# 24 instead of 20 ranges of edges scattered to blocks; low source numbers spread by DMA; attribute products in 64-row halves

## What is computed

```python
h = relu(layernorm(x))
x = x + gcn(relu(gcn(h, W1, b1)), W2, b2)       # two GCN convolutions over the edges
h = relu(layernorm(x))
msg  = relu(concat(h[row], edge_attr) @ L1_W1 + b1)     # one message per edge
agg  = segment_sum(msg, col) / max(count, 1)
out  = x + relu(concat(h, agg) @ L1_W2 + b2)
```

## Time and profile before

| | |
|---|---|
| median of 3 runs | 2926.35 us (2925.55 to 2926.58) |
| the profiled execution | 2923.46 us |
| its span in the profile | 2921.6 us |
| mean granted clock of TensorE | 0.954 |
| busy share of the span | PE 87%, POOL 63%, DVE 55%, ACT 35% |

### The profile page before, as it was taken

The page is one execution under the profiler, slowest core; times in us unless marked ns, Lnnn a source line. Parts: engine busy times, 40 slices in busy tenths (PEclk is TensorE's granted clock), DMA queues, the critical chain, the costliest instruction groups (busy, mean ns, idle before and its releaser), DMA issues.

```text
span 2921.6 us, 53392 instructions
## 1 busy us (share of the span) xinstructions
PE 2554.8 (87%) x18818; PEld 2059.8 (71%) x18819; DVE 1612.8 (55%) x3028; ACT 1021.3 (35%) x2891; POOL 1842.2 (63%) x1747
## 2 busy tenths in 40 slices
PE   1756578999999995999996599999999999999997
PEld 0104357888778894888885487877878777777786
DVE  7889897888766556000002654544545455454556
ACT  6504133566667764000000233333333333333331
POOL 2852363677887771756661277777777777777750
PEclk9997699999999997989998699999999999999999
DMA  9102221332434442746563222232222232222321
GB/s 372 37 6 74 77 63 59 133 124 106 150 116 153 177 180 89 237 155 239 210 231 113 89 76 79 76 90 77 79 76 80 79 88 79 76 79 76 90 49 48
DMA packets 111653, 327.75 MB, mean 112 GB/s; under 512 B 33282, under 2 KB 71527, under 8 KB 104855
## 3 DMA queue, kind: packets, MB, share of 16 engines
q10 hardware_dynamic: 6624, 147.72, 12.6%
q0 software_dynamic: 58352, 93.38, 12.4%
q1 hardware_dynamic: 46377, 82.75, 8.1%
HBM read 197.11 MB, written 126.61 MB: 111 GB/s over the span
## 4 chain that ended last, share of the span: by engine, by line
PE 71%; DVE 18%; issue 5%; POOL 2%; ACT 2%; DMA 1%; DVEq 1%; ACTq 0%; SPq 0%; POOLq 0%
PE ps_feat L889 12%; PE ps_node L889 12%; PE ps_extra L1036 7%; PE ps_sum L997 7%; PE ps_pre L990 6%; DVE region_c L1680 4%; DVE region_c L1676 4%; PE ps_node L1020 3%; PE ps_node L1024 3%; PE ps_pre L877 3%; PE ps_sum L1020 2%; PE ps_feat L1020 2%; PE ps_sum L1024 2%; PE ps_feat L1024 2%; PE ps_turn L1012 2%
## 5 line engine op out<-in xcount | busy, mean ns | idle before, releaser
L630 POOL DMA_INDIRECT rows<-table,region_a x928 | 895.6, 965 | 384.7 <-issue 262.4
L648 POOL DMA_INDIRECT permuted<-edge_rows_of,slot_of_edge x640 | 728.1, 1138 | 323.0 <-issue 150.6
L889 PE MATMUL ps_node<-region_a,region_b 128*128 128x256 bf16 x3528 | 450.5, 273 | 1.8 <-ACT region_b L1126 1.8
L1849 DVE TENSOR_SCALAR region_b<-ps_turn,consts 128x512 f32<-128x512 f32 (+1 forms) x280 | 191.6, 684 | 461.8 <-PE ps_turn L1012 418.4
L889 PE MATMUL ps_feat<-region_a,region_b 128*128 128x256 bf16 x3528 | 445.8, 273 | 0.0
L889 PEld LDWEIGHTS ps_node<-region_a,region_b 128*128 128x128 bf16 x3528 | 341.4, 97 | 45.4 <-ACT region_b L1126 2.0
L889 PEld LDWEIGHTS ps_feat<-region_a,region_b 128*128 128x128 bf16 x3528 | 342.3, 98 | 44.1
L1680 DVE TENSOR_TENSOR region_c<-iota_key,region_c 128x1568 bf16<-128x1568 f16 (+1 forms) x324 | 354.1, 1093 | 0.0
L1676 DVE TENSOR_TENSOR region_c<-iota_units,region_c 128x1024 bf16<-128x1024 bf16 x324 | 224.3, 692 | 136.5 <-PE ps_turn L877 91.3
L1164 ACT ACTIVATE region_a<-ps_pre 128x392 bf16<-128x392 f32 x384 | 190.8, 497 | 215.8 <-PE ps_pre L877 207.9
L1036 PE MATMUL ps_extra<-region_b 128*128 128x128 f32 x1960 | 265.2, 275 | 0.0
(11 more groups left out here) (255 smaller groups left out, 3747.1 us busy)
## 6 DMA issues: line engine op xcount, KB each, us to landing
counts<-region_a ACTq DMA_DIRECT2D x24, 3136.0 KB
region_a<-counts ACTq DMA_DIRECT2D x22, 3136.0 KB
permuted<-region_b SPq DMA_DIRECT2D x21, 833.0 KB, 23.6
region_a<-permuted SPq DMA_DIRECT2D x20, 833.0 KB, 4.7
region_a<-attr_t_in SPq DMA_DIRECT2D x58, 256.0 KB
rows<-table,region_a POOLq DMA_INDIRECT x928
edge_rows_of<-edge_cols_in POOLq DMA_DIRECT2D x20, 544.0 KB
permuted<-edge_rows_of,slot_of_edge POOLq DMA_INDIRECT x640
```

What stands on the lines that cost most here:

```text
L630: nc.gpsimd.indirect_dma_start(rows[:, s, j * D:(j + 1) * D], None, tables[2], bass.IndirectOffsetOnAxis(ap=message_rows[:, c * TC + j:c * ...
L648: nc.gpsimd.indirect_dma_start(permuted, bass.IndirectOffsetOnAxis(ap=slot_of_edge[:, r * RT + k:r * RT + k + 1], axis=0), edge_rows_of[:, ...
L889: ins = mm(strip_bank(buf), parts[:, h, k], counts[buf][:, h], start=(h == 0 and k == 0), stop=(h == SB - 1 and k == PARTS - 1), skip_grou ...
L1849: v.tensor_scalar(source_hot[u % 2][:, 0:n], ps_turn[:, 0:n], partition, None, ALU.is_equal).then_inc(B["source"], 1)
```

## The change

- `RANGES` 20 becomes 24. Twelve pairs instead of ten, 768 scatters instead of 640 (`PACED` 16 and 8 ranges), 25 clearing transfers instead of 21, and 200 chunks (800 gathers) instead of 232 (928). A pair has 16 chunks; the last has 24.
- The low source numbers no longer go through `spread`. Once a range, PE transposes them (`turn_lows`), ACT copies the result out and stores it to DRAM, and four DMAs on ACT's queue (`load_lows`) bring it to all partitions as bfloat16 in `spread_lo`, from which `source` reads. `spread_lo` is one buffer, filled for one range after the other, a part as soon as its units are compared.
- `products_of` makes two chunks at a time, each as two matmuls of 64 rows by 256 columns, whose results lie in different PSUM banks.
- SP loads the blocks of the next pair when ACT has staged and DVE has prepared the old ones, and no longer when DVE has compared them. Some semaphores are merged.

```diff
-RANGES = 20
+RANGES = 24
+LO_UNITS = 4
+LO_TURNED_AT = (7, DU + 10)
+LO_LOADED_AT = ({DU - 4: (0, 1), DU - 2: (2,), DU: (3,)}, {2 * DU - 1: (0, 1), 2 * DU: (2,), 2 * DU + 1: (3,)})
-PAIR_TURNS = 3
+PAIR_TURNS = 2
-PACED = (13, 7)
+PACED = (16, 8)
...
                 def products_of(k, c):
-                    s = c % SLOTS
-                    if s % HALF == 0:
-                        pe.wait_ge(attr_loaded[s // HALF], (k * PAIR_TURNS + c // SLOTS) * 16 + 16)
-                    pe.wait_ge(rows_added, k * PAIR_CHUNKS + c + 1)
-                    mm(ps_pre[s % 2][:], attr[:, s], edge_w[:].rearrange("p j d -> p (j d)"), start=True, stop=True).then_inc(pre_ready, 1)
+                    pe.wait_ge(rows_added, k * PAIR_CHUNKS + c + 2)
+                    if c % HALF == 0:
+                        pe.wait_ge(attr_loaded[c % SLOTS // HALF], (k * PAIR_TURNS + c // SLOTS) * 16 + 16)
+                    for q in range(2):
+                        for half in range(2):
+                            part = slice(half * P // 2, (half + 1) * P // 2)
+                            last = mm(pre_halves[:, half, q], attr[part, (c + q) % SLOTS],
+                                      edge_w[part, half * 2:half * 2 + 2].rearrange("p j d -> p (j d)"), start=True, stop=True)
+                    last.then_inc(pre_ready, 2)
...
+                def turn_lows(k, r):
+                    pe.wait_ge(B["prepared"], k * 2 + r + 1)
+                    pe.wait_ge(B["lo_evicted"], k * 2 + r + 1)
+                    mm(ps_turn[0:SB, 0:P], block_lo[r][:, 0:SB], ident_bf[:], start=True, stop=True).then_inc(B["lo_turned"], 1)
...
-                    pe.wait_ge(B["source"], k * PAIR_UNITS + u + 1)
-                    for j in range(n):
-                        last = mm(ps_turn[:, j * P:(j + 1) * P], block_lo[r][:, b0 + j:b0 + j + 1].to_broadcast([P, P]), ident_bf[:],
-                                  start=True, stop=True)
-                    last.then_inc(B["spread"], 1)
...
+                def store_lows(k, r, stored=True):
+                    act.wait_ge(B["lo_turned"], k * 2 + r + 1)
+                    if stored:
+                        act.wait_ge(B["lo_stored"], (k * 2 + r) * 16)
+                    nc.scalar.activation(lo_turned[:], ps_turn[0:SB, 0:P], ACT.Copy).then_inc(B["lo_evicted"], 1)
+                    act.wait_ge(B["lo_evicted"], k * 2 + r + 2)
+                    act.dma_start(lo_dram[r].rearrange("(b e) -> b e", e=P), lo_turned[:]).then_inc(B["lo_stored"], 16)
+
+                def load_lows(k, r, i, sourced=None):
+                    act.wait_ge(B["lo_stored"], (k * 2 + r) * 16 + 16)
+                    if sourced is not None or i >= 2:
+                        act.wait_ge(B[f"lo_loaded_{i % 2}"], (k * 2 + r) * 32 + i // 2 * 16)
+                    if sourced is not None:
+                        act.wait_ge(B["source"], sourced)
+                    first, end = i * LO_BLOCKS * P, min((i + 1) * LO_BLOCKS, SB) * P
+                    act.dma_start(spread_lo[:, first:end], lo_dram[r:r + 1, first:end].to_broadcast([P, end - first])
+                                  ).then_inc(B[f"lo_loaded_{i % 2}"], 16)
...
-                    v.tensor_scalar(source_hot[u % 2][:, 0:n], ps_turn[:, 0:n], partition, None, ALU.is_equal).then_inc(B["source"], 1)
+                    v.tensor_scalar(source_hot[u % 2][:, 0:n], lows, partition, None, ALU.is_equal).then_inc(B["source"], 1)
```

More of the change, by code:

```diff
@@ L99 @@
 assert SEG % BANKS == 0
-assert DT % (SLOTS * TC) == 0 and LAST_CHUNKS == 2 * SLOTS and RANGES % 2 == 0 and DU % 2 == 0 and sum(UNIT_TILES) == SB and RT % 2 == 0
+assert DT % (SLOTS * TC) == 0 and LAST_CHUNKS % SLOTS == 0 and RANGES % 2 == 0 and DU % 2 == 0 and sum(UNIT_TILES) == SB and RT % 2 == 0
 assert DT * P >= RANGE_ROWS
@@ L292, in build @@
         ps_extra = ps("ps_extra", [P, 512])
-        ps_pre = [ps("ps_pre0", [P, 512]), ps("ps_pre1", [P, 512])]
+        pre_banks = ps("pre_banks", [P, 1024])
+        ps_pre = [pre_banks[:, k * 512:(k + 1) * 512] for k in range(2)]
+        pre_halves = pre_banks[:].rearrange("p (k h c) -> p k h c", k=2, h=2)
         ps_turn = ps("ps_turn", [P, 512])
@@ L338, in build @@
         rows_staged = [sem("rows_staged_0"), sem("rows_staged_1")]
-        scattered = [sem(f"scattered_{j}") for j in range(4)]
-        lo_ready = sem("lo_ready")
-        hi_ready = sem("hi_ready")
+        scattered = [sem(f"scattered_{j}") for j in range(2)]
+        hot_ready = sem("hot_ready")
         hist_used = sem("hist_used")
@@ L1042, in pair_of @@
                         c = chunk_of(u, chunks)
-                        if c is not None and (not last or c + 2 < chunks):
+                        if c is not None and c % 2 == 0 and (not last or c + 2 < chunks):
                             products_of(k, c + 2)
                         if u < PAIR_UNITS:
-                            spread(k, u)
+                            turn_attr(k, u)
                         if c is not None:
@@ L1052, in pair_of @@
                             block_sums(k, u - 2)
+                        if u == LO_TURNED_AT[0]:
+                            turn_lows(k, 1)
+                        if u == LO_TURNED_AT[1] and not last:
+                            turn_lows(k + 1, 0)
+                turn_lows(0, 0)
                 pe.wait_ge(B["msgs"], 2)
                 products_of(0, 0)
-                products_of(0, 1)
                 with pe.Fori(0, PAIRS - 1) as k:
@@ L1250, in pair_of @@
                             block_message(k, u - 1)
+                        if u == LO_TURNED_AT[0] + 1:
+                            store_lows(k, 1)
+                        for i in LO_LOADED_AT[0].get(u, ()):
+                            load_lows(k, 1, i, k * PAIR_UNITS + (min(LO_UNITS * (i + 1), DU) + 1))
+                        if u == LO_TURNED_AT[1] + 1 and not last:
+                            store_lows(k + 1, 0)
+                        for i in LO_LOADED_AT[1].get(u, ()):
+                            if not last:
+                                load_lows(k + 1, 0, i, k * PAIR_UNITS + (DU + min(LO_UNITS * (i + 1), DU) + 1))
+                for j in range(2):
+                    act.wait_ge(scattered[j], RANGES // 2 * RT * 16)
+                store_lows(0, 0, False)
+                for i in range(LO_PARTS):
+                    load_lows(0, 0, i)
                 stage_attr(0, 0)
@@ L1432, in _ @@
                         dve.wait_ge(hist_used, i * 2 + s + 1)
[L1433 removed]
+                        for hot, of, n in ((hot_lo, dst_lo, P), (hot_hi, dst_hi, NB)):
                             v.tensor_tensor(hot[:, s], iota_bf[:, None, 0:n].to_broadcast([P, HT, n]),
                                             of[:, bass.ds(i * (2 * HT) + s * HT, HT)].unsqueeze(2).to_broadcast([P, HT, n]),
[L1436 removed]
+                                            ALU.is_equal).then_inc(hot_ready, 1)
                 dve.wait_ge(count_ready, 1)
@@ L1845, in source @@
                 def source(k, u):
-                    n = unit_tiles(u % DU)[1] * P
-                    dve.wait_ge(B["spread"], k * PAIR_UNITS + u + 1)
+                    first, n = (a * P for a in unit_tiles(u % DU))
+                    lows = spread_lo[:, first:first + n]
+                    i = u % DU // LO_UNITS
+                    dve.wait_ge(B[f"lo_loaded_{i % 2}"], (k * 2 + u // DU) * 32 + (i // 2 * 16 + 16))
                     dve.wait_ge(B["pre"], k * PAIR_UNITS + u + 1)
-                    v.tensor_scalar(source_hot[u % 2][:, 0:n], ps_turn[:, 0:n], partition, None, ALU.is_equal).then_inc(B["source"], 1)
+                    v.tensor_scalar(source_hot[u % 2][:, 0:n], lows, partition, None, ALU.is_equal).then_inc(B["source"], 1)
                 def target(k, u):
@@ L1858, in products_in @@
                 def products_in(k, c):
-                    add_products(c % SLOTS, k * PAIR_CHUNKS + c, (k * PAIR_TURNS + c // SLOTS + 1) * (16 * TC))
+                    dve.wait_ge(pre_ready, k * PAIR_CHUNKS + (c // 2 * 2 + 2))
+                    dve.wait_ge(e["gathered"][c % SLOTS], (k * PAIR_TURNS + c // SLOTS + 1) * (16 * TC))
+                    halves = rows[:, c % SLOTS].rearrange("p (k c) -> p k c", k=2)
+                    v.tensor_tensor(halves, halves, pre_halves[:, :, c % 2], ALU.add).then_inc(rows_added, 1)
                 def pair_of(k, chunks, last):
```

51 lines of the change are left out of this document (28 added, 23 removed).

## The result

The kernel after takes 2875.84 us (median of 4 runs, 2873.84 to 2881.52), the kernel before 2925.95 beside it (2923.59 to 2926.58): ratio 0.9833, interval 0.9816 to 0.985. The profiled execution took 2875.38 us, 48.1 less than the one the sum was made against.

What follows compares the result with a forecast made beforehand. PE's instructions plus loop ends were taken to bound the messages, DVE's ranking setup. 105.9 - 65.5 + 2.6 - 49 + 27.0 - 4 + 2 = +19.0 us on 2923.5; forecast 2945, range 2932 to 2957 (8 in 10: 2905 to 2978).

Steps and rivals of the forecast that it cites:

- What bounds the kernel: Messages: PE's instructions plus loop ends, 116.8 + 6.2 us a pair, POOL level but not ahead; setup: DVE's ranking.
- The loop ends: Repeated ends of the message loop: 6.2 us each, ten instead of eight, +12.4 us.
- late lows: Loop ends waiting for lows: +2 us in the sum; as a rival +60, 3005 us, chance 0.05.
- Prices of PE's work: PE in the messages: units without spread at 2.80 and 2.15 us; dropping the spread -65.5, transposes of lows +2.6.
- the group of halves: Message products of two chunks on PE: 1.23 us a group, a gain of 0.49, -49 us in all.
- Whole overlap: Rival: half products run side by side at all times, 0.86 us a group, 2908 us, faster; chance 0.24.
- drains on either side: Rival: PE drains before and after each group of half products, 1.50 us a group, 2972 us; chance 0.13.
- no overlap: Rival: half products do not overlap, the group stays at 1.72 us, +49, 2994 us; chance 0.07.
- POOL's lag: Rival: POOL lags in the convolutions by more than its 20 us cover, +10 to +30, 2965 us; chance 0.05.
- Ranks: Setup on DVE: ranking four more ranges delays the first convolution by 27.0 us.
- Scatters: Convolutions on POOL: 128 more scatters cost 0, ending 55 to 80 us after the first convolution's windows, some 20 us cover.
- Start of the messages: First one-hot ready near 1664; staging behind DMAs +2 us, late gathers of the first pair gone -6, sum -4.

Runs made afterwards that it cites:

- 20 ranges: The kernel after with 20 ranges and 928 gathers as before, keeping lows by DMA and products in halves: 2925.53 us, ratio 1.0018 to the kernel before.

## Why the prediction was wrong

- **What bounds the kernel: failed in part.** It saw that POOL's gathers take as long as a pair (about 120 us) and let the chain decide for PE. But the chain names whoever came last, by however little. There were two bounds within 1.5 us of each other a pair: POOL 121.8, PE 116.8 + 6.2. Both had to go for anything to be gained (fewer gathers alone 5 us, loops written out alone 7, both 48). That 128 gathers go "gives nothing by itself" is nearly true, and 20 ranges show what it hides: without it the cheaper PE work gives nothing at all.
- **The loop ends: the step that failed.** "Twelve pairs have ten repeated loop ends instead of eight: 2 x 6.2 = +12.4." The price was read from the kernel before and carried over as a constant. It belongs to the bodies of its loops, which the change shortens: at 1449 and 273 records no loop end stops an engine, and doubled bodies bring the stops back. Ten ends at nothing are 62 us less, and of the 2 us for late lows 1 came: 19 - 63 = -44 against -48.1 measured. That this is so near is in part luck. The messages came out 7 us lower still (5 of them in pairs of 92.9 us instead of 93.4), and the time before them 4 us higher. The prediction named this as a way to be wrong in sign ("if the loop end costs less than 6 us with POOL no longer full") and gave it no chance of its own; its condition was not the cause either, for with POOL slack and the bodies of before an end still costs 5.3. "PE stands 2.1 us without work" was half of the stop: DVE's (3.40 us) ended last and held the chain, as the run with PE's loop alone written out shows.

The Trainium skill states the rule on its page "Runtime: NRT & Kernel Launch", in "Instruction fetch mechanics": a taken branch to code outside the engine's current window waits for a fetch. The packets above follow it. By the page's sizes, 512 instructions for most engines and 2048 for PE, both bodies of before are short enough; by the runs a PE body of 1754 and DVE bodies of 371 and 347 paid, PE bodies up to 1658 and DVE bodies up to 297 did not. The measurement decides.

- **Prices of PE's work: right for the kernel after.** Units without the spread came at 2.75 to 2.80 and 2.10 to 2.15 us (2.80, 2.15), the group of halves at 0.50 less (0.49), its mechanism refuted. The work of before was priced some 0.6 us a pair too low and the loop end as much too high (117.4 and 5.3, where it had 116.8 and 6.2); removing the spread was worth 84 us, with what else changed beside it, and not 63.
- **The rivals.** Whole overlap gave the sign but not the cause: the group gained 0.50, not 0.86. Of drains on either side, no overlap and late lows none came as priced; POOL's lag was real and 2.5 us long.
- **Ranks: right.** +27.4 against +27.0.
- **Scatters: right in cost, not in lag.** POOL's scatters of the first convolution ended at 1236.9, some 108 us after the windows, not 55 to 80; the cover of 20 us was used up and 2.5 us showed. From the first `bn_stats` to the first message product +3.5 in all, where 0 was predicted.
- **Start of the messages: right in place, not in size.** DVE's first one-hot was at 1695.77, the add that waited for the gather beside it at 1695.16. From the first message product to the end of the first pair it took 109.7 us instead of 135.4; less the work of a pair (92.9 and 117.4) that is 1.2 us saved, where the terms for it make 4.

## What to carry over

When two engines need the same time for a period, the chain shows one of them, and an edit that relieves one is worth little (here 5 or 7 us of 48): set each engine's own need for a period beside the period, and ask of a bundle of edits whether it relieves all. A fixed cost at a loop end is a function of the loop body on each engine: before carrying it over, count the body's instructions before and after, and look at the page's instruction packets. A releaser that the chain names need not be what the engine waited for: look up in the code what its wait asks for. A price that enters a sum ten times deserves a rival of its own.

## What the hardware showed

- Loop ends in the messages cost 5.3 us each with bodies of 1754 (PE) and 371 (DVE) records and POOL slack, some 0.3 with 1575 and 297, and none that the chain shows with 1449 and 273. Each stop of PE goes with some nine instruction packets.
- A stop of 2 to 3 us costs its own length where the clock stays full (1.98 and 2.95 us cost 1.9 and 2.9), and 3.3 to 7.5 where it does not: behind the stops PE's clock was granted at 1.2 GHz for 3.4 to 10.2 us, in the kernel before mostly for 6.8.
- Half products in two row halves take 1.07 us a group of eight records in either order of issue, and the next transpose's spacing is 0.24 instead of 0.11.
- A gather every 1.27 us is POOL's pace when nothing holds it: 0.97 us busy and 0.28 of "issue" by the group before (836.7 and 244.1 over 867).
